# Attend matmuls of a token tile in one piece, turned probabilities kept in the probabilities' own buffer

## The reference, cut to what matters

```
xn = layernorm(x)
Q = xn @ W_q.T ; K = ctx @ W_k.T ; V = ctx @ W_v.T          # 16 heads of 32
scores = Q K^T / sqrt(32) - slope[head] * (query_pos - key_pos), masked
e = exp(scores - max)
attn = e / (1 + sum(e))
x = x + tanh(g_xattn) * ((attn @ V) @ W_o.T)
xn = layernorm(x); xr, xk = mixes of xn with xn of the token before
x = x + tanh(g_ffn) * sigmoid(xr @ W_r.T) * (relu(xk @ W_k.T)^2 @ W_v.T)
```

## Time and profile before

| what | value |
|---|---|
| median of 3 runs | 1523.69 us |
| lowest and highest | 1522.95 and 1523.78 us |
| span of the profiled execution (first to last instruction) | 1519.6 us |
| median less that span | 4.1 us |
| granted TensorE clock, mean | 0.999 |
| PE busy | 1442.7 us (95%), 10864 matmuls |
| DVE, ACT, POOL busy | 1161.5, 889.5, 721.3 us |

### The profile page before, as it was taken

One profiled execution on the slowest core, in us unless ns is written; L12 is line 12 of the kernel. 1 busy time (PEld: TensorE's weight loads), 2 busy tenths in 40 slices (PEclk: granted clock), 3 DMA queues, 4 the chain that ended last, 5 costly groups with the idle time before them and its releaser, 6 DMA issues.

```text
span 1519.6 us, 32873 instructions
## 1 busy us (share of the span) xinstructions
PE 1442.7 (95%) x10864; PEld 1083.1 (71%) x10864; DVE 1161.5 (76%) x2889; ACT 889.5 (59%) x2928; POOL 721.3 (47%) x766
## 2 busy tenths in 40 slices
PE   7988899999999999999999999999999999999998
PEld 6876767677676767667686766767676676768667
DVE  4456868787887868798786879878687887868775
ACT  5147474665747465574747566473756657475662
POOL 0003455545455555545555464545546454555542
PEclk9999999999999999999999999999999999999999
DMA  8721001020200102020010202011020101001000
GB/s 270 215 66 49 8 29 50 0 76 0 56 20 28 49 0 76 0 56 20 28 49 14 62 0 56 20 36 41 14 62 0 56 20 53 23 27 50 1 30 28
DMA packets 53009, 65.95 MB, mean 43 GB/s; under 512 B 23024, under 2 KB 29168, under 8 KB 52976
## 3 DMA queue, kind: packets, MB, share of 16 engines
q1 hardware_dynamic: 52976, 65.52, 14.6%
HBM read 40.87 MB, written 24.64 MB: 43 GB/s over the span
## 4 chain that ended last, share of the span: by engine, by line
PE 48%; DVE 34%; issue 11%; ACT 3%; DMA 2%; DVEq 1%; SPq 0%; POOL 0%; ACTq 0%; POOLq 0%
PE rotating L401 33%; DVE probs L1038 7%; PE probs_bank L561 5%; DVE diff L1100 4%; PE score_bank L460 4%; DVE mix_k L1095 4%; PE attn_bank L575 3%; DVE relu L1100 3%; DVE square L1095 2%; PE score_bank L401 2%; ACT probs L773 2%; DVE mask_in L1137 2%; DVE stats L1008 2%; DVE norm L1017 2%; DVE xs L1064 2%
## 5 line engine op out<-in xcount | busy, mean ns | idle before, releaser
L773 ACT ACTIVATE probs<-probs,neg_max 128x120 f32<-128x120 f32 x1024 | 391.2, 385 | 29.6 <-DVE neg_max L1042 29.6
L1320 POOL TENSOR_TENSOR probs<-probs,recip 128x960 f32<-128x960 f32 x128 | 229.7, 1794 | 237.5 <-DVE recip L1053 237.5
L401 PE MATMUL rotating<-mixed_key,w_key 128*128 128x512 f32 x720 | 205.0, 413 | 24.8 <-ACT gated L825 24.8
L401 PE MATMUL rotating<-w_proj,attn_t 128*128 128x512 f32 x768 | 220.9, 417 | 2.9 <-DVE xnt_or_act L1023 2.0
L781 ACT COPY probs_t<-probs_bank 120x512 f32<-120x512 f32 x256 | 149.8, 585 | 121.3 <-PE probs_bank L561 121.1
L1038 DVE SCALAR_TENSOR_TENSOR probs<-mask_in,score_bank 128x120 f32<-128x120 f32 x1024 | 213.0, 269 | 9.5 <-PE score_bank L460 9.5
L401 PE MATMUL rotating<-w_value,xnt_or_act 128*128 128x512 f32 x720 | 202.3, 409 | 10.2 <-DVE xs L1064 10.2
L401 PE MATMUL rotating<-w_gate,mixed_gate 128*128 128x512 f32 x768 | 209.7, 409 | 0.0
L401 PE MATMUL rotating<-xnt_or_act,w_query 128*128 128x256 f32 x1536 | 198.7, 286 | 0.5 <-DVE xnt_or_act L1023 0.5
L773 ACT ACTIVATION_READ_ACCUMULATOR probs<-probs,neg_max 128x1 f32 x1024 | 194.0, 189 | 0.0
L401 PEld LDWEIGHTS rotating<-xnt_or_act,w_query 128*128 128x128 f32 x1536 | 187.7, 191 | 1.9 <-DVE xnt_or_act L1023 0.8
(11 more groups left out here) (126 smaller groups left out, 2167.7 us busy)
## 6 DMA issues: line engine op xcount, KB each, us to landing
xs<-in_x_dram SPq DMA_DIRECT2D x64, 256.0 KB, 2.9
out_dram<-gated SPq DMA_DIRECT2D x64, 256.0 KB, 3.0
value_scratch<-gated SPq DMA_DIRECT2D x16, 240.0 KB, 2.6
mask_in<-in_mask_dram SPq DMA_DIRECT2D x16, 240.0 KB, 2.6
keys_t<-key_scratch SPq DMA_DIRECT2D x16, 240.0 KB, 3.6
values<-value_scratch SPq DMA_DIRECT2D x16, 240.0 KB, 3.8
probs<-in_ctx_t_dram SPq DMA_DIRECT2D x6, 480.0 KB, 7.0
key_scratch<-query_t SPq DMA_DIRECT2D x12, 240.0 KB, 5.1
```

The source lines that it names most:

```text
L401: mm = pe.matmul(bank, stationary(a, c), moving(b, c), start=(i == 0), stop=(i == MATMULS - 1))
L773: e = act.activation(probs[:, t % 2, head, :], probs[:, t % 2, head, :], ACT.Exp, bias=neg_max[:, t % 2, head:head + 1], accum_out=sums[:, ...
L1320: pool.tensor_tensor(part, part, recip[:, t % 2, heads].unsqueeze(2).to_broadcast((P, H // 2, NK)), ALU.mult)\
```

## The change

`probs` is widened from 120 to 128 columns a head, and `probs_t` is gone. ACT writes the turned probabilities of a group (120 partitions, 128 columns a head) over the probabilities that were just transposed. All reads and writes of untransposed probabilities take the first 120 columns of a head. In `with_attention` all four `attend` calls come after the last portion, the portions are 3, 3, 3 and 3, and `attend` waits once, for all four copies of the tile. DVE's `bias` waits for `attn_done` of the tile two before, in place of `probs_turned`. The context loads of the start use the front part of the widened buffer.

```diff
-        probs = sb("probs", [P, 2, H, NK])
-        probs_t = sb("probs_t", [NK, 2, J, P])
+        probs = sb("probs", [P, 2, H, P])
...
-                    mm = pe.transpose(probs_bank[0:NK, j * P:(j + 1) * P], probs[:, t % 2, g * J + j, :], ident[:])
+                    mm = pe.transpose(probs_bank[0:NK, j * P:(j + 1) * P], probs[:, t % 2, g * J + j, 0:NK], ident[:])
...
             def attend(b, t, g):
-                pe.wait_ge(probs_t_ready, (b * QT + t) * G + g + 1)
                 if g == 0:
+                    pe.wait_ge(probs_t_ready, (b * QT + t) * G + G)
...
-                                   values[:, head * HD:(head + 1) * HD], probs_t[:, g % 2, j, :],
+                                   values[:, head * HD:(head + 1) * HD], probs[0:NK, t % 2, head, :],
...
-                def with_attention(t, what, tile, portions=(4, 3, 3, 2)):
+                def with_attention(t, what, tile, portions=(3, 3, 3, 3)):
                     at = 0
                     for g in range(G):
                         turn_probs(b, t, g)
                         use(what, tile, range(at, at + portions[g]))
                         at += portions[g]
-                        if g > 0:
-                            attend(b, t, g - 1)
-                    attend(b, t, G - 1)
+                    for g in range(G):
+                        attend(b, t, g)
...
-                    e = act.activation(probs[:, t % 2, head, :], probs[:, t % 2, head, :], ACT.Exp,
+                    e = act.activation(probs[:, t % 2, head, 0:NK], probs[:, t % 2, head, 0:NK], ACT.Exp,
...
-                act.copy(probs_t[:, g % 2], probs_bank[0:NK, :].rearrange("k (j q) -> k j q", j=J))\
+                act.copy(probs[0:NK, t % 2, g * J:(g + 1) * J, :], probs_bank[0:NK, :].rearrange("k (j q) -> k j q", j=J))\
...
-                        dve.wait_ge(probs_turned, (b * QT + t - 1) * G)
+                        dve.wait_ge(attn_done, b * QT + t - 1)
...
-                part = probs[:, t % 2, heads, :]
+                part = probs[:, t % 2, heads, 0:NK]
```

More of the change, by code:

```diff
@@ L138, in flamingo_block @@
         wv_split = mixed_gate
-        ctx_raw = probs[:].rearrange("p a h k -> p (a h k)").rearrange("p (a c k) -> p a c k", a=4, k=CK)
+        ctx_raw = probs[:].rearrange("p a h k -> p (a h k)")[:, 0:4 * 4 * CK].rearrange("p (a c k) -> p a c k", a=4, k=CK)
         ctx_split = [xnt_or_act[:].rearrange("p s c t -> p (s c t)")[:, i * 2 * CT * CK:(i + 1) * 2 * CT * CK]
@@ L1037, in bias @@
                     head = g * J + j
-                    z = dve.scalar_tensor_tensor(out=probs[:, t % 2, head, :], in0=neg_dist[:, t, :], scalar=SLOPES[head],
+                    z = dve.scalar_tensor_tensor(out=probs[:, t % 2, head, 0:NK], in0=neg_dist[:, t, :], scalar=SLOPES[head],
                                                  in1=score_banks[j][:, g * NK:(g + 1) * NK], op0=ALU.mult, op1=ALU.add)
@@ L1041, in bias @@
                 dve.wait_ge(scores_biased, (b * QT + t) * G + g + 1)
-                dve.tensor_reduce(neg_max[:, t % 2, g * J:(g + 1) * J], probs[:, t % 2, g * J:(g + 1) * J, :],
+                dve.tensor_reduce(neg_max[:, t % 2, g * J:(g + 1) * J], probs[:, t % 2, g * J:(g + 1) * J, 0:NK],
                                   AX.X, ALU.max, negate=True).then_inc(max_ready, 1)
```

## The result

The changed kernel takes 1534.41 us (median of 4, 1532.63 to 1534.79) against 1523.38 for the kernel before (median of 4): a ratio of 1.0069, 95% interval 1.0057 to 1.0081. That is 11.0 us slower, inside the range and on the forecast side; 16 had been forecast.

The account below looks back on a forecast made before the run. No engine alone bounds it: PE and DVE hand the end over inside each batch. Tiles 0 and 1 lose 0.85 + 0.19 = 1.04 us, 16 with the first batch: 1519.6 + 16 + 4.1 = 1539.7 us, range 1531 to 1548.

Parts of the forecast that it names:

- The round of the bank: Transposes, ACT's copy, next transposes through the one probs_bank: 1.33 us, against 1.13 of PE work, so PE waits 0.2.
- The path to the end: PE lateness in tiles 0 and 1 reaches the end in full; in tiles 2 and 3 only beyond 0.7 us.
- PE alone: A tile's stretch on PE without waits: 5.80 us against 6.28, 0.48 less from two fewer attend runs.
- The run of attends: All 16 heads of a tile in one run on PE: 1.17 us, with 0.27 for four more heads.
- the +0.19 of tile 1: Tile 1's stretch on PE grows by 0.19 us, to 6.46 to 6.50, through its bank rounds and attends.
- Tile 0: Third copy, behind act_split(1) waiting for POOL, still starts 3.95 us in; the stretch becomes 7.13 against 6.28, +0.85 us.
- The wait at value 3: PE's wait for DVE's residual of tile 2 falls from 0.7 to about 0.3 us, covering 0.42 of lateness.
- Costs taken as nothing: DVE's new wait, the copy's writes, and the maximum and POOL's multiplication skipping 8 columns a head: all taken as 0.
- The 4.1 us around the span: Time outside the profiled span, added to 1535.6 us to reach the forecast 1539.7.
- that rival: Faster, chance 0.12: tiling-mode changes on PE decide, 0.48 us won a tile; 1509 us, or 1493 if tiles 2 and 3 count.
- No change: Lateness is taken up further on, as the 0.7 us at value 3 would do: 1524 us, chance 0.08.
- slower still: The 0.42 us of tiles 2 and 3 isn't covered, as ACT comes late for DVE: 6.3 more, 1546, chance 0.14.

Follow-up runs that it names:

- half_copy: The changed kernel with ACT copying only the second 64 of each head's 128 columns, leaving out half the turned probabilities: 1518.21 us, ratio 0.9964.
- layout_only: The widened buffer and copies into it, with attends woven in as in the kernel before (portions 4, 3, 3, 2): 1524.24 us, ratio 1.0006.
- wait_each: The changed kernel, but each of the four attend groups waits for its own copy: 1533.66 us, ratio 1.0065.
- split_behind: The changed kernel with ACT's act_split(1) of tile 0 moved behind the third copy: 1526.6 us, ratio 1.002.
- fill_tile0: fill_rounds with only tile 0 given four products a round, tiles 1 and 2 put back to three: 1518.63 us, ratio 0.9969.
- fill_rounds: split_behind with four products in each round of tiles 0, 1 and 2, four steps borrowed from a neighbour: 1510.06 us, ratio 0.9916.
- fill_exps: fill_rounds with ACT's second group of tile 2's exponentials before attn_out(1), and DVE's attn_low(1) behind tile 2's reciprocals: 1499.81 us, ratio 0.9846.
- exps_before: The kernel before with only the swap of fill_exps on ACT and DVE: 1509.21 us, ratio 0.9911.

## Why the prediction was right, and where its sizes were off

**The round of the bank: right, its exact size partly by luck.** 1.33 us was forecast as 0.66 + 0.59 + 0.08, from rows of the kernel before in which the round was hidden. It is measured as 0.69 + 0.59 + 0.05 (in tile 1 of the changed kernel transposes at 746.99, their copy at 747.68, the next transposes at 748.32), so two errors of 0.03 us cancel. half_copy shows that the round goes through the copy. The first round of a tile is 1.27 to 1.29 in tiles 1 to 3, not 1.30: transposes follow a copy by 0.05 us when PE has long been waiting, where I had taken 0.08 from a row in which it was just arriving.

**The path to the end: right.** Lateness in tiles 0 and 1 reaches the end in full. In every kernel that leaves ACT's and DVE's lists behind tile 1 alone, a batch changed by as much as the end of tile 1's attends did, counted from tile 0's first transposes (median over the 14 batches in the loop, and mean length of these batches, us):

| kernel | tile 1's attends end | against before | batch | against before |
|---|---|---|---|---|
| before | 23.47 | | 87.84 | |
| layout_only | 23.48 | +0.01 | 87.84 | 0.00 |
| changed | 24.20 | +0.73 | 88.55 | +0.71 |
| wait_each | 24.06 | +0.59 | 88.38 | +0.54 |
| split_behind | 23.62 | +0.15 | 87.98 | +0.14 |
| half_copy | 23.23 | -0.24 | 87.57 | -0.27 |
| fill_tile0 | 23.15 | -0.32 | 87.48 | -0.36 |
| fill_rounds | 22.68 | -0.79 | 87.04 | -0.80 |

In half_copy tile 2 won 0.6 us and tile 3 lost 0.4, and neither shows in the batch. The swap of fill_exps and exps_before works on the link behind, so these two are not in the table.

**PE alone: right.** 1.13 us between transposes and a stretch of 5.80 were forecast; half_copy has 1.13 and 5.65, lower by the run of attends.

**The run of attends: mis-sized, the term that failed.** "all 16 in one run take 1.17" is 1.01. The row of eight heads held a short wait for the fourth copy. This is 0.16 us a tile, in each of tiles 0 and 1: with the first round's 0.03 it makes the +0.19 of tile 1 into 0. In tile 0 it makes +0.85 into +0.69, and two small errors lead to the measured 0.73: the fourth transposes came 0.04 sooner than forecast (4.59 us into the tile, not 4.63), and the attends 1.41 behind them, not 1.33. 15 x (1.04 - 0.72) = 4.8 us, which is the distance between 16 forecast and 11 measured. The forecasts of 6.5 us for tiles 1 to 3 and of a little over 1 us a batch missed by the same term: 6.28 and 0.71. So one piece did win on PE what it lost in the rounds, in three tiles of four.

**Tile 0: right in place and cause.** The third copy starts 3.96 us into the tile, 3.95 forecast. split_behind takes 0.6 of the 0.7 us away.

**Waits.** "PE before had none" of the waits for copies is nearly right: PE has a single one in the kernel before, of 1.3 us. PEld's rows name the copy before 99 runs of attends, 36.2 us in total, but that is 0.37 us each, as much as before the 93 whose idle time is put to no engine (33.9 us), so they are no sign of lost time. The one that mattered, in the run of eight, is too short to stand in any list of waits. The wait at value 3 stayed at 0.7, not 0.3, because tiles 2 and 3 were not late after all; so that slack was never called on.

**Costs taken as nothing: right.** Layout, stride, DVE's new wait and the copy's new place, by layout_only.

**The 4.1 us around the span** are not of the kernel. Each run of the changed kernel took 1.8 us more than its span (1534.48 and 1532.7); by that measure the profiled execution of the kernel before was 2.3 us shorter than its median. The forecast of 16 us doesn't use them.

**The rivals.** The rule that a change of tiling mode drains the array (Trainium skill, TensorEngine Tiling (Array Packing), Tiling Modes) was priced by rows at 0.48 us a tile; the traces agree with a gain of this kind, 0.63 with half a copy (0.48 and the 0.16 of the run of attends make 0.64), and show that it is not to be had while a copy is waited for. No run separates a drain from what else the start of a run may cost. The 1493 us of that rival don't follow from its own prices: 15 x 4 x 0.48 = 29 us give 1495. "No change" was refuted by the time and by the table above, "slower still" by tiles 2 and 3 at 6.28 us.

## What to carry to other kernels

Before small operations are gathered into one piece, look at what they were covering: here each group of attends hid part of a copy out of a single PSUM bank. Give each round as much work as its copy needs (four products here, not three), and only then collect. Whether filled rounds with the attends still woven in would do as well was not tested. Look in each engine's list for an item that waits for something slow and stands ahead of something urgent: two such places gave 0.57 us (`act_split(1)`, which cost time only after the change) and 1.06 us a batch (`attn_out(1)`), where the change cost 0.71. And ask at which point of a batch the time passes to the next engine: here it was the end of tile 1's attends, and what tiles 2 and 3 won or lost did not count.

## What was not expected of the hardware

A semaphore wait that is satisfied cost PE nothing that shows: 16 heads in one run took 1.01 us with one wait and with four. A group of transposes took 0.64 us from its start to ACT's copy when its first weight load on PEld stands ahead of its first matmul (738.25 and 738.89 in the kernel before, load at 738.02). It took 0.69 when both start together: behind a wait (746.99 and 747.68 in the changed kernel), but behind an attend without a wait too (741.21 and 741.90 in the kernel before). In the first and the last batch, which stand outside the hardware loop, the stretch of tile 1 took 6.46 us in the changed kernel where inside the loop it was 6.28; the kernel before had 6.29 and 6.30 there. The difference lies where PE waits for a copy: in the last batch tile 1's second transposes start 0.14 us after the end of the copy (1454.73 + 0.59, then 1455.46), and in the loop 0.05. No run here explains it.
